# Chosen keys and values brought together by TensorE products with one-hot rows instead of indirect DMA gathers

## The chip, the core and the metric

The kernel runs on one core of a Trainium2 chip. The metric is the time of one execution on the device in microseconds (us), the median of several runs. Lower is better.

## What is computed

One transformer block over 2048 tokens of width 128: a layer norm with a modulation, sparse attention with 16 heads of width 8, then a mixture of eight experts. What matters here is the attention. A small router gives every token a score for every head; in each head only the 819 tokens with the highest scores serve as keys and values (`k_keep`), and all 2048 tokens are queries.

```python
h1 = jax.nn.relu(hidden_states @ r_w1.T + r_b1)
routing_logits = jax.nn.sigmoid(h1 @ r_w2.T + r_b2)
routing_scores = jax.nn.sigmoid(routing_logits)
attn = jnp.einsum('bhqd,bhkd->bhqk', q, k) / jnp.sqrt(jnp.float32(D))
k_keep = max(1, int(tgt_len * SPARSITY))
_, top_idx = jax.lax.top_k(jnp.transpose(routing_scores, (0, 2, 1)), k_keep)
...
sparse = jnp.where(keep[:, :, None, :], attn, NEG_INF)
w = jax.nn.softmax(sparse.astype(jnp.float32), axis=-1).astype(q.dtype)
out = jnp.einsum('bhqk,bhkd->bhqd', w, v)
```

## The kernel before

All five engines run programs written out by hand that meet at semaphores; no scheduler orders anything. The kernel has three parts.

**Ahead of the attention.** Layer norm, the router, keys and values `KV` (tokens on partitions, 32 columns a head pair), queries `QP` in three bf16 parts that sum to the f32 value, and a search in 11 rounds on DVE for each head's threshold. DVE then has, for each token and head, its place among the chosen (L911). From there the chosen keys have to be packed: 819 keys a head make 6 full blocks of 128 and a rest of 51, and the rests of the two heads of a pair (`i`, 0 to 7) share a block, so a pair has `STEPS` = 13 blocks.

To pack them, DVE makes one-hot columns (`columns`, `onehot`, L925 to L939), PE multiplies them (`index_mm`, L1293, then `row_to_partition`, L1304), ACT copies (L684), and DVE writes the row numbers `idx` (`index`, L945). `KV` has meanwhile gone to DRAM (`kv_dram`, L440). POOL then issues one indirect DMA a block (`gathers`, L535), 13 a pair, each fetching 128 rows of 16 f32 values into `G`. `prep` adds the bias and splits the keys into bf16 parts in `KS` (on DVE for pair 0, L972 to L989, on POOL for the others, L552 to L569), `prep_v` puts the values in `VS`, and PE turns `KS` into `KT` (L1413 for pair 0, `turn_k`, L1351, later).

**The attention loop.** A chunk is 512 queries of one pair; there are `NCH` = 32 chunks, four a pair (`NQ`). Two streams run side by side. One finds the largest score of each query: 16 "units" a chunk, each a product of 128 queries with half a head's keys (`score_unit`, L1338 to L1343) into one of three PSUM banks (`RING`) and a maximum over it on DVE (L997). It runs ahead by `LEAD` = 28 units, so that chunk n's loop holds the units of chunks n+1 and n+2. The maxima are split in three bf16 parts by `split_max` in three steps on DVE (L1007, L1011, L1014), turned by PE (`turn_m`, L1357), copied by ACT (`copy_mt`, L695) and carried by SP's DMA into rows of `QS` (`m_rows`, L459). The other stream is the weighting: in `KSTEPS` = 7 steps k, PE computes scores with keys on partitions less the maximum (`scores`, L1382, ended by row parts of `QS`), ACT takes exp (`weights`, L722) into `PR`, and PE multiplies by the values into `OP` (`weigh`, L1398; `weigh_shared`, L1406). ACT copies `OP` to `OS`, PE sums and turns it (`turn_o`, L1362, into a corner of `ST`), ACT copies that (`copy_ot`, L713). PE's program fixes where each of these stands in the row.

POOL's loop over pairs (L585 on) is: `weighted(i - 3)`, which divides a finished pair's output and so waits for DVE's `REC` (L591), then `gathers(i)`, `prep(i)`, `prep_v(i)`. So pair i's gathers (i of 3 and more) are issued from the end of the second chunk of pair i-2 on; those of pairs 0 and 1 stand ahead of the loop, pair 2's at its start. After its last `idx` is ready SP also loads the 4 MB of expert weights (`WE`, L467).

**The tail.** Second layer norm, expert routing, a scatter to slots in DRAM, 24 expert tiles, and a scatter-add to the output.

## Time and profile before

| | us |
|---|---|
| median of 3 runs | 628.78 |
| lowest and highest | 625.04, 629.18 |
| the profiled execution | 629.86 |
| its span in the trace | 628.1 |
| mean granted TensorE clock | 0.793 |

A time of a row is counted from the start of the span. The profiled execution is 1.08 us above the median, and 1.76 us of it lie outside the span.

### The profile page before, as it was taken

To read this page: it belongs to the slowest core of one execution; us is meant where nothing else is said; L and a number is where in the kernel's file an instruction comes from. 1 tells how busy PE (TensorE), PEld (TensorE's weight loads), DVE (VectorE), ACT (ScalarE), POOL (GpSimd) and SP (SyncE) were. 2 spreads that over 40 slices of the span, in tenths; PEclk is the share of its full clock that TensorE was granted. 3 is DMA by queue.
4 is the path that set the end of the run, shared out by engine and by line. 5 is a ranking of instruction groups with operands and counts; after the bars stand their busy time and mean duration, and the time that the engine had idled before them with its cause. 6 is when DMAs were issued, how large, how long until landed. Compare 5 with 4: busy or idle time off the path is not lost.

```text
span 628.1 us, 9542 instructions
## 1 busy us (share of the span) xinstructions
PE 473.5 (75%) x3286; PEld 228.0 (36%) x3286; DVE 392.0 (62%) x1042; ACT 311.9 (50%) x447; POOL 208.6 (33%) x282
## 2 busy tenths in 40 slices
PE   4666526588999599789879969969999976007994
PEld 4334425222333134223223323323434326006993
DVE  8787402675888378468648748737888955202552
ACT  3333000025778267358546637726877873005662
POOL 4100875072003701720640360171000300540886
PEclk9886555557999689779858869878999995557997
DMA  7625000034000010000001001000000001140331
GB/s 229 104 102 147 10 6 4 0 116 160 2 27 3 6 27 2 8 1 28 6 4 27 2 7 28 2 6 12 16 3 2 1 16 54 34 117 18 28 28 12
DMA packets 26346, 22.04 MB, mean 35 GB/s; under 512 B 6272, under 2 KB 22464, under 8 KB 26304
## 3 DMA queue, kind: packets, MB, share of 16 engines
q1 hardware_dynamic: 15632, 16.56, 8.8%
q0 software_dynamic: 7296, 2.96, 4.3%
q10 hardware_dynamic: 3376, 1.98, 1.8%
q8 instruction: 23, 0.38, 0.2%
q14 instruction: 19, 0.16, 0.1%
HBM read 12.89 MB, written 8.93 MB: 35 GB/s over the span
## 4 chain that ended last, share of the span: by engine, by line
PE 58%; DVE 15%; issue 11%; POOL 6%; another core or an unknown queue 5%; ACT 2%; DMA 2%; POOLq 0%; DVEq 0%; SPq 0%; ACTq 0%
PE OP L1398 16%; PE ST L1382 12%; PE SC L1340 6%; DVE tile_max L997 6%; PE ST L1362 5%; POOL out L629 4%; PE SC L1338 4%; PE SC L1293 4%; DVE PR L863 2%; PE OP L1406 2%; POOL slots_dram L621 2%; DMA KV<-slots_dram 1%; PE OP L1479 1%; PE ST L1500 1%
## 5 line engine op out<-in xcount | busy, mean ns | idle before, releaser
L997 DVE TENSOR_REDUCE tile_max<-SC 128x1 f32<-128x410 f32 (+1 forms) x512 | 272.5, 577 | 106.8 <-PE SC L1338 50.8
L722 ACT ACTIVATE PR<-ST 128x1024 f32<-128x1024 f32 (+1 forms) x224 | 209.0, 962 | 84.4 <-PE ST L1382 48.7
L535 POOL DMA_INDIRECT G<-kv_dram,idx x104 | 108.4, 1042 | 79.0 <-DVE idx L945 44.3
L1382 PE MATMUL ST<-QS,KT 51*128 51x512 bf16 (+1 forms) x416 | 118.0, 415 | 12.1 <-issue 7.2
L1398 PE MATMUL OP<-PR,VS 128*32 128x512 f32 x768 | 116.7, 683 | 0.4 <-ACT PR L722 0.4
L1338 PE MATMUL SC<-KT,QS 48*128 48x410 bf16 x256 | 82.7, 378 | 9.8 <-issue 6.2
L1340 PE MATMUL SC<-KT,QS 48*128 48x409 bf16 x128 | 48.8, 381 | 11.5 <-issue 7.6
L1382 PEld LDWEIGHTS ST<-QS,KT 51*128 51x128 bf16 (+1 forms) x416 | 30.7, 98 | 68.6 <-issue 56.6
L1342 PE MATMUL SC<-KT,QS 48*128 48x358 bf16 x128 | 44.6, 348 | 9.9 <-DVE tile_max L997 8.0
L629 POOL DMA_INDIRECT out<-PR,owner x24 | 37.7, 1569 | 28.7 <-issue 27.7
L591 POOL TENSOR_TENSOR XN<-OTS,REC 128x128 f32<-128x128 f32 x14 | 5.5, 414 | 117.0 <-DVE REC L1020 117.0
L1362 PE MATMUL ST<-C,OS 128*128 128x32 f32 x248 | 39.6, 285 | 0.2
L578 POOL COPY VS<-G 128x48 f32<-128x48 f32 x8 | 1.8, 224 | 113.7 <-PE OP L1398 95.7
L1338 PEld LDWEIGHTS SC<-KT,QS 48*128 48x128 bf16 x256 | 19.4, 96 | 50.6 <-DVE tile_max L997 29.6
L1362 PEld LDWEIGHTS ST<-C,OS 128*128 128x128 f32 x248 | 32.9, 194 | 11.6 <-issue 10.8
L1340 PEld LDWEIGHTS SC<-KT,QS 48*128 48x128 bf16 x128 | 12.1, 94 | 66.8 <-DVE tile_max L997 50.4
L695 ACT ACTIVATE MT<-ST 24x128 bf16<-24x128 bf16 x32 | 8.5, 267 | 52.7 <-remote 26.5
L1293 PE MATMUL SC<-ABUF,B 128*14 128x64 f16 x256 | 27.5, 296 | 6.4 <-DVE ABUF L939 3.4
L1500 PE MATMUL ST<-C,KV 128*128 128x128 f32 x24 | 5.9, 428 | 33.9 <-DMA KV<-slots_dram 33.9
L684 ACT ACTIVATE by_code<-SC 14x64 f32<-14x64 f32 x16 | 3.4, 214 | 54.4 <-remote 26.0
L621 POOL DMA_INDIRECT slots_dram<-ABUF,slot x16 | 15.6, 976 | 43.3 <-DVE slot L1163 38.7
L1293 PEld LDWEIGHTS SC<-ABUF,B 128*14 128x14 f16 x256 | 24.0, 109 | 8.8 <-issue 7.4
(240 smaller groups left out, 581.4 us busy)
## 6 DMA issues: line engine op xcount, KB each, us to landing
kv_dram<-KV SPq DMA_DIRECT2D x4, 512.0 KB, 2.9
WE<-in_w_fc SPq DMA_DIRECT2D x1, 2048.0 KB
WE<-in_w_proj SPq DMA_DIRECT2D x1, 2048.0 KB
G<-kv_dram,idx POOLq DMA_INDIRECT x104
slots_dram<-zeros ACTq DMA_DIRECT2D x1, 1548.0 KB, 11.5
KV<-slots_dram SPq DMA_DIRECT2D x1, 1548.0 KB, 7.4
q_parts_dram<-QP SPq DMA_DIRECT2D x3, 512.0 KB, 3.7
QS<-q_parts_dram SPq DMA_DIRECT2D x16, 96.0 KB
```

The lines of the kernel that those rows point to most:

```text
L535: pool.indirect_dma_start(G[:, i % 2, slot_of(s), :], None, kv_dram, bass.IndirectOffsetOnAxis(ap=idx[:, i, s:s + 1].bitcast(U32), axis=0) ...
L621: pool.indirect_dma_start(slots_dram, bass.IndirectOffsetOnAxis(ap=slot[:, t:t + 1].bitcast(U32), axis=0), XN2[:, t, :], None, bounds_chec ...
L629: pool.indirect_dma_start(out[0], bass.IndirectOffsetOnAxis(ap=owner[:, n:n + 1].bitcast(U32), axis=0), YS[:, n, :], None, bounds_check=L ...
L722: nc.scalar.activation(PR[:, k, 0:cols], ST[:, (KSTEPS * n + k) % 2, 0:cols], ACT.Exp, scale=float(D) ** -0.5).then_inc(exp_done, 1)
L997: v.tensor_reduce(tile_max[:, n % 2, at_col:at_col + 1], bank(RING_AT["unit", u])[:, 0:410 - f], AX.X, ALU.max).then_inc(s_reduced, 1)
L1293: last = mm(tokens_of(i)[0][32 * e:32 * e + CODES, :], B1[:, 2 * i + e, t, :], A1[:, i % 2, e, :, t], start=(t == 0), stop=(t == NT - 1), ...
L1338: last = mm(to[:, 0:410], q, KT[rows, i % 2, 0:410], start=True, stop=True)
L1340: last = mm(to[:, 0:409], q, KT[rows, i % 2, 410:KEEP], start=True, stop=True)
L1342: mm(to[:, 0:358], q, KT[rows, i % 2, 410:768], start=True, stop=True)
L1362: last = mm(turned_o(n)[:, 32 * t:32 * t + 32], OS[:, P * t:P * t + P], cc("sum_groups"), start=True, stop=True)
L1382: last = mm(ST[:, at_step % 2, 512 * e:512 * e + 512], KT[rows, i % 2, P * tile:P * tile + P], QS[rows, i % 2, CHUNK * c:CHUNK * (c + 1)], ...
L1398: last = mm(OP[32 * g:32 * g + 32, :], VS[:, i % 2, tile, :], PR[:, k, 512 * e:512 * e + 512], start=first, stop=False, skip_group_check=True)
```

## The change

`kv_dram`, the gathers and the row numbers are gone. A head's 819 keys and values are now brought together on PE: for each of the 16 tiles of 128 tokens there is one product. Its stationary operand is a 128x128 f32 one-hot matrix (token by row within a block), and its moving operand the tile's 16 key and value columns, repeated for each block that the tile can reach and multiplied by 0 or 1 (`masked`), 16 to 112 columns wide; all 16 sum up in one PSUM tile of 112 columns (`bring`). The two heads no longer share the rest block while packing: `SLOTS` = 14.

DVE builds both operands for pair 0. POOL builds them for all others: a head needs four differences of 512 elements a partition, two comparisons of 1024, and three masked products of 256, 896 and 320 (`distances`, `onehot`, `masked`). The operands of pairs 2 to 7 are built during the loop, a half or a whole step beside each chunk (four POOL pieces a pair). The products of pairs 0 and 1 (heads (0,0), (0,1), (1,0), (1,1)) stand ahead of the loop, (1,0) after unit 17 and (1,1) after unit 27. Those of pairs 2 to 7 stand in chunks 1 to 23: 16 in chunk 1, 8 in each of the others, half of them at k=3 and half at k=4. ACT copies the sum out of PSUM (`copy_g`), and `weigh` waits for that, since the sum lies in `OP`'s bank. `turn_o` writes to that bank also, so `weigh` waits for ACT's copy of it, too.

Moved: the second and third step of `split_max` go from DVE to POOL; `turn_m` goes ahead of `turn_o` at k=3; the first `weigh` goes from k=4 to k=5. SP loads `WE` after (1,1) is brought, not after the last `idx`. Buffers of POOL's operands share `ABUF`, `WE` and `QBUF`; the last covers `QP`.

```diff
+FIRST_HALF, SECOND_HALF = range(0, NT // 2), range(NT // 2, NT)
+BRING = {1: (2, 0, range(NT), 0), 2: (2, 1, FIRST_HALF, 0), 3: (2, 1, SECOND_HALF, 1)}
+for p in range(3, NP):
+    for n, (e, part) in enumerate(((0, 0), (0, 1), (1, 0), (1, 1))):
+        BRING[4 * p - 8 + n] = (p, e, [FIRST_HALF, SECOND_HALF][part], part)
...
+        def keys_of(p, e):
+
+            if p == 0:
+                return SC[:, 2 * e, 0:BLOCKS * 2 * D]
+            if p == 1:
+                return ST[:, 1, 512 * e:512 * e + BLOCKS * 2 * D]
+            return OP[:, P:P + BLOCKS * 2 * D]
...
-            for g in range(4):
-                sp.wait_ge(kv_ready, 2 * g + 2)
-                sp.dma_start(kv_t[:, 4 * g:4 * g + 4, :], KV[:, 4 * g:4 * g + 4, :]).then_inc(kv_out, 16)
...
-            sp.wait_ge(idx_ready, NP)
+            sp.wait_ge(g_done, brought(1, 1))
...
-            def gathers(i, tiles=range(STEPS), fetched=gathered):
-                pool.wait_ge(idx_ready, i + 1)
-                if i >= 2:
-                    pool.wait_ge(v_ready, i)
-                    pool.wait_ge(o_norm, 2 * (i - 2))
-                for s in tiles:
-                    pool.indirect_dma_start(
-                        G[:, i % 2, slot_of(s), :], None, kv_dram,
-                        bass.IndirectOffsetOnAxis(ap=idx[:, i, s:s + 1].bitcast(U32), axis=0),
-                        bounds_check=L * H - 1, oob_is_err=False).then_inc(fetched, 16)
...
+            def distances(p, e, first=0, last=NT):
+
+                if p >= 2 and first == 0:
+                    pool.wait_ge(g_done, brought(p - 1 if p > 2 else 0, e))
+                for t in range(first, last, 4):
+                    nc.gpsimd.tensor_tensor(
+                        onehot_of(p, e)[:, t:t + 4, :], cc("place").rearrange("p (a q) -> p a q", a=1).to_broadcast([P, 4, P]),
+                        row_of[:, t:t + 4, 2 * p + e:2 * p + e + 1].to_broadcast([P, 4, P]), ALU.subtract).then_inc(hot_step, 1)
+                    done = next_hot()
+                return done
+
+            def onehot(p, e, done, first=0, last=NT):
+                pool.wait_ge(hot_step, done)
+                for t in range(first, last, 8):
+                    words = onehot_of(p, e)[:, t:t + 8, :]
+                    nc.gpsimd.tensor_scalar(words, words, 0.0, None, ALU.is_equal).then_inc(built, 1)
+
+            def masked(p, e):
+                h = 2 * p + e
+                for t0, t1, b0, b1 in RUNS[e]:
+                    shape = [P, t1 - t0, b1 - b0, 2 * D]
+                    nc.gpsimd.tensor_tensor(
+                        masked_of(p, e)[:, t0:t1, b0:b1, :],
+                        KV[:, t0:t1, 2 * D * h:2 * D * (h + 1)].rearrange("p t (b c) -> p t b c", b=1).to_broadcast(shape),
+                        mask[:, t0:t1, h, b0:b1].rearrange("p t (b c) -> p t b c", c=1).to_broadcast(shape),
+                        ALU.mult).then_inc(built, 1)
+
...
+            def split_max(n):
+
+                part = NMB.rearrange("p (e a t w) -> p e a t w", e=2, a=PARTS, w=2)[:, :, :, :, 1]
+                pool.wait_ge(m_chain, n + 1)
+                nc.gpsimd.tensor_tensor(NM[:, :, 1, :], NM[:, :, 0, :], part[:, :, 0, :], ALU.subtract).then_inc(m_rest, 1)
+                pool.wait_ge(m_rest, n + 1)
+                nc.gpsimd.tensor_tensor(NM[:, :, 2, :], NM[:, :, 1, :], part[:, :, 1, :], ALU.subtract).then_inc(m_split, 1)
...
+                nc.gpsimd.tensor_tensor(g, g, G[:, b, 1, :, :], ALU.add).then_inc(k_step, 1)
...
-            gathers(0, range(EARLY), gathered_early)
-            gathers(0, range(EARLY, STEPS), gathered_late)
-            gathers(1)
-            prep(1)
...
-            for i in range(2, NP):
-                if i >= 3:
-                    weighted(i - 3)
-                gathers(i)
-                prep(i)
-                prep_v(i)
...
+            pool.wait_ge(bias_in, 16)
+            pool.wait_ge(built0, 10)
+            pool.wait_ge(mask_ready, 2)
+            pool.wait_ge(kv_ready, NT // 2)
+            onehot(1, 0, distances(1, 0))
+            masked(1, 0)
+            onehot(1, 1, distances(1, 1))
+            split_max(0)
+            masked(1, 1)
             pool.wait_ge(prepared0, 2)
             prep_v(0)
...
+            pool.wait_ge(qparts_out, 16 * PARTS)
+            for n in range(NCH):
+                i, c = n // NQ, n % NQ
+                if n == 0:
+                    even = distances(2, 0)
+                if n + 1 < NCH:
+                    split_max(n + 1)
+                if c == 0 and i + 1 < NP:
+                    prep(i + 1)
+                    prep_v(i + 1)
+                    if n == 0:
+                        onehot(2, 0, even)
+                        masked(2, 0)
+                    if i + 2 < NP:
+                        onehot(i + 2, 1, distances(i + 2, 1, 0, 8), 0, 8)
+                elif c == 1 and i + 2 < NP:
+                    onehot(i + 2, 1, distances(i + 2, 1, 8, NT), 8, NT)
+                    masked(i + 2, 1)
+                elif c == 2:
+                    if i >= 1:
+                        weighted(i - 1)
+                    if i + 3 < NP:
+                        onehot(i + 3, 0, distances(i + 3, 0, 0, 8), 0, 8)
+                elif c == 3 and i + 3 < NP:
+                    onehot(i + 3, 0, distances(i + 3, 0, 8, NT), 8, NT)
+                    masked(i + 3, 0)
...
+            def copy_g(p, e, part, number):
+
+                act.wait_ge(g_done, number)
+                if p == 0 and e == 0:
+                    act.wait_ge(init_pool, 1)
+                if p >= 2:
+                    act.wait_ge(v_ready, 3 * (p - 1))
+                src = keys_of(p, e).rearrange("p (b c) -> p b c", b=BLOCKS)
+                to = G[:, p % 2, part, :, :]
+                if e == 0:
+                    nc.scalar.activation(to[:, 0:13:2, :], src, ACT.Copy).then_inc(g_copied, 1)
+                else:
+                    nc.scalar.activation(to[:, 1:12:2, :], src[:, 1:, :], ACT.Copy).then_inc(g_first, 1)
+                    nc.scalar.activation(to[:, 13, :], src[:, 0, :], ACT.Copy).then_inc(g_copied, 1)
...
-                if n >= 1:
-                    act.wait_ge(otr_done, n)
                 if n + 1 < NCH:
                     copy_mt(n + 1)
+                if n in BRING:
+                    act.wait_ge(g_done, brought_by(n))
                 if n >= 1:
                     copy_ot(n - 1)
+                if n in BRING:
+                    p, e, tiles, part = BRING[n]
+                    copy_g(p, e, part, brought_by(n))
                 weights(n, 4, 3)
                 weights(n, 5, 4)
...
+            masks(0, 2)
+            dve.wait_ge(kv_ready, NT // 2)
+            dve.wait_ge(mask_ready, 1)
+            for e in range(2):
+                onehot(e)
+                masked(e)
...
+            def bring(p, e, tiles, begins=True, ends=True):
+
+                if p == 0:
+                    pe.wait_ge(built0, 5 * (e + 1))
+                else:
+                    pe.wait_ge(built, 5 * (2 * (p - 1) + e + 1))
+                for t in tiles:
+                    b0, b1 = reach(t, e)
+                    last = mm(keys_of(p, e)[:, 2 * D * b0:2 * D * b1], onehot_of(p, e)[:, t, :],
+                              masked_of(p, e)[:, t, b0:b1, :].rearrange("p b c -> p (b c)"),
+                              start=(begins and t == tiles[0]), stop=(ends and t == tiles[-1]), skip_group_check=True)
+                return last
...
-                    if k == 5 and n >= 1:
-                        pe.wait_ge(ot_ready, n)
...
+                    pe.wait_ge(v_ready, 3 * (i + 1))
                     if n >= 1:
-                        pe.wait_ge(o_copied, n)
+                        pe.wait_ge(ot_ready, n)
+                    pe.wait_ge(g_copied, brought_by(n))
...
+            bring(0, 1, range(NT)).then_inc(g_done, 1)
+            turn_first(0, SC[0:64, 1, :])
...
+            for u in range(12, 18):
                 score_unit(u)
-            pe.wait_ge(q_ready, 4 * PARTS)
+            bring(1, 0, range(NT)).then_inc(g_done, 1)
+            for u in range(18, LAST[0] + 5):
+                score_unit(u)
             turn_m(0)
             for u in range(LAST[0] + 5, LEAD):
                 score_unit(u)
...
+                    scores(n, k, 0 if k == 3 else e, True)
+                    unit()
                     if k == 3:
-                        scores(n, k, 0, True)
+                        if n + 1 < NCH:
+                            turn_m(n + 1)
                         unit()
                         if n >= 1:
                             turn_o(n - 1, (0, 1))
-                        unit()
-                        if n >= 1:
+                            unit()
                             turn_o(n - 1, (2, 3))
-                        if n + 1 < NCH:
-                            turn_m(n + 1)
+                        if n in BRING:
+                            p, e_, tiles, part = BRING[n]
+                            bring(p, e_, tiles[:len(tiles) // 2], ends=False)
                         continue
-                    scores(n, k, e, True)
-                    unit()
                     scores(n, k, 1 - e, False)
+                    if k == 4 and n in BRING:
+                        p, e_, tiles, part = BRING[n]
+                        bring(p, e_, tiles[len(tiles) // 2:], begins=False).then_inc(g_done, 1)
+                    if k == 5:
+                        weigh(n, (0, 1), first=True)
+                    if k == 6:
+                        weigh_shared(n)
                     unit()
                     if k == 1:
...
                     if k == 2 and n % NQ == 1 and n // NQ + 1 < NP:
                         turn_k(n // NQ + 1)
-                    if k == 4:
-                        weigh(n, (0, 1), first=True)
-                        unit()
-                    if k == 5:
-                        weigh_shared(n)
+                while units:
+                    unit()
                 weigh(n, (2, 4))
```

What stands in PE's row in a chunk, from k=3 to the first `weigh`. Before (`ST<-QS,KT` are `scores`, `SC<-KT,QS` units, `OS` is `turn_o`, `NM` is `turn_m`, `OP<-PR,VS` is `weigh`):

```order
L1362 MATMUL ST<-C,OS 128x32 x2
L1357 MATMUL ST<-identb,NM 24x128
L1382 MATMUL ST<-QS,KT 128x512
L1338 MATMUL SC<-KT,QS 128x410
L1382 MATMUL ST<-QS,KT 128x512
L1342 MATMUL SC<-KT,QS 128x358
L1343 MATMUL SC<-KT,QS 128x51
L1398 MATMUL OP<-PR,VS 32x512 x4
```

And of the change, in a chunk whose first eight tiles are brought (`OP<-QBUF,ABUF` are the products of `bring`):

```order
L1377 MATMUL ST<-identb,NM 24x128
L1358 MATMUL SC<-KT,QS 128x410
L1382 MATMUL OP<-C,OS 128x32 x2
L1358 MATMUL SC<-KT,QS 128x410
L1382 MATMUL OP<-C,OS 128x32 x2
L1325 MATMUL OP<-QBUF,ABUF 128x32
L1325 MATMUL OP<-QBUF,ABUF 128x48
L1325 MATMUL OP<-QBUF,ABUF 128x64
L1325 MATMUL OP<-QBUF,ABUF 128x80
L1400 MATMUL ST<-QS,KT 128x512
L1362 MATMUL SC<-KT,QS 128x358
L1363 MATMUL SC<-KT,QS 128x51
```

`turn_m` now stands ahead of both parts of `turn_o`; four products follow them, and after the next two `scores` come four more.

POOL's row for one pair in the loop before (`G` gathered, then the bias and the split into `KS`):

```order
L535 DMA G<-kv_dram,idx 128x16 x13
L552 TENSOR_TENSOR G<-G,BG 128x208
L556 CAST KS<-G 128x13x24
L558 TENSOR_TENSOR KR<-G,KS 128x104
L560 CAST KS<-KR 128x13x16
L562 TENSOR_TENSOR KR<-KR,KS 128x104
```

And in the change, from the end of `prep` in a pair's first chunk to the second `split_max` after it (`ABUF` one-hot rows, `QBUF` masked columns, `NM` `split_max`):

```order
L601 COPY VS<-G 128x7x8
L602 COPY VS<-G 128x6x8
L603 COPY VS<-G 128x8
L536 TENSOR_TENSOR ABUF<-C,row_of 128x512 x2
L546 TENSOR_SCALAR ABUF<-ABUF 128x1024
L562 TENSOR_TENSOR NM<-NM 128x2x4
L564 TENSOR_TENSOR NM<-NM 128x2x4
L536 TENSOR_TENSOR ABUF<-C,row_of 128x512 x2
L546 TENSOR_SCALAR ABUF<-ABUF 128x1024
L552 TENSOR_TENSOR QBUF<-KV,mask 128x4x80
L552 TENSOR_TENSOR QBUF<-KV,mask 128x896
L552 TENSOR_TENSOR QBUF<-KV,mask 128x4x64
```

The 13 DMAs are gone; elementwise work of each chunk stands between one chunk's `split_max` and the next one's.

## Rows read from the trace of the kernel before

**Rows 1.** Busy time of each engine in stretches (us, instructions), PEclk, DMA share, GB/s.
```profile
208.00:224.00 16.00, 9.72 (x47) 2.27 (x43) 6.06 (x12) 5.37 (x7) 8.91 (x14) 0.50 0.06 5
432.00:448.00 16.00, 15.89 (x131) 6.49 (x131) 14.25 (x34) 12.49 (x19) 0.82 (x4) 1.00 0.10 26
```
**Rows 2.** Timeline of ACT, `copy_mt` alone: start, us, what, idle before.
```profile
196.21 0.27 ACT L695 ACTIVATE MT<-ST 24x128 bf16<-24x128 bf16 x1 [0.69 <-PE ST L1362]
209.87 0.27 ACT L695 ACTIVATE MT<-ST 24x128 bf16<-24x128 bf16 x1 [3.04 <-remote]
227.87 0.27 ACT L695 ACTIVATE MT<-ST 24x128 bf16<-24x128 bf16 x1 [0.86 <-PE ST L1362]
```
**Rows 3.** Timelines: POOL's split beside DVE's maxima, then one pair's gathers on POOL.
```profile
155.89 0.58 DVE L997 TENSOR_REDUCE tile_max<-SC 128x1 f32<-128x409 f32 x1
...
156.02 0.38 POOL L558 TENSOR_TENSOR KR<-G,KS 128x104 f32<-128x104 f32 x1
...
199.05 1.06 POOL L535 DMA_INDIRECT G<-kv_dram,idx  x1 [0.85 <-POOL XN L591]
...
214.76 1.00 POOL L535 DMA_INDIRECT G<-kv_dram,idx  x1 [0.30 <-issue]
```
**Rows 4.** Timeline, all engines, from the places to the loop's first `scores`.
```profile
53.59 0.62 DVE L925 TENSOR_TENSOR WE<-key_of,C 128x448 f16<-128x448 f16 x1
...
61.88 2.95 POOL L535 DMA_INDIRECT G<-kv_dram,idx  x1 [44.34 <-DVE idx L945]
...
102.10 0.87 POOL L558 TENSOR_TENSOR KR<-G,KS 128x104 f32<-128x104 f32 x1
...
114.48 0.85 PE L1413 MATMUL SC<-identb,KS 128*64 128x128 bf16 x6 [2.19 <-DVE RS L989]
...
116.24 0.50 PE L1338 MATMUL SC<-KT,QS 48*128 48x410 bf16 x1 [0.80 <-DVE KT L991]
...
135.74 0.61 PE L1382 MATMUL ST<-QS,KT 51*128 51x512 bf16 x1 [1.61 <-DMA QS<-MT]
```
**Rows 5.** Timeline of PE and DVE in a chunk without gathers.
```profile
468.37 0.39 PE L1382 MATMUL ST<-QS,KT 51*128 51x512 bf16 x1
...
472.01 0.63 PE L1362 MATMUL ST<-C,OS 128*128 128x32 f32 x4
...
472.58 0.34 PE L1338 MATMUL SC<-KT,QS 48*128 48x410 bf16 x1
...
477.85 0.39 PE L1382 MATMUL ST<-QS,KT 51*128 51x512 bf16 x1
...
471.60 0.16 DVE L1007 TENSOR_REDUCE NM<-tile_max 128x8 f32<-128x16 f32 x1
```
**Rows 6.** A stretch of the tail, a PE row, and groups by form (the first from 432 to 500).
```profile
592.00:608.00 16.00, 16.00 (x142) 15.84 (x142) 10.19 (x27) 10.50 (x18) 13.37 (x9) 1.00 0.35 30
...
566.98 5.94 PE L1500 MATMUL ST<-C,KV 128*128 128x128 f32 x24 [33.91 <-DMA KV<-slots_dram]
...
L1340 PEld LDWEIGHTS SC<-KT,QS 48*128 48x128 bf16 x28 | 2.6, 92 | 12.1 <-DVE tile_max L997 12.1
...
L615 POOL TENSOR_TENSOR KV<-XN,gate 128x448 f32<-128x448 f32 x4 | 4.4, 1138 | 0.1
L1044 DVE TENSOR_TENSOR X<-KV,X 128x1792 f32<-128x1792 f32 x1 | 2.0, 2018 | 0.0
...
L521 POOL CAST place<-C 128x1024 f16<-128x1024 f32 x1 | 1.0, 1037 | 0.1
```
**Rows 7.** The load of `WE`: SP's issue, a stretch, the second chunk's first `scores`.
```profile
134.98 0.57 SPq L467 DMA_DIRECT2D WE<-in_w_proj  x1
...
148.00:150.00 2.00, 2.00 (x13) 0.27 (x9) 1.10 (x3) 1.02 (x1) 0.62 (x1) 0.50 0.13 46
...
150.39 0.60 PE L1382 MATMUL ST<-QS,KT 51*128 51x512 bf16 x1
```

405 lines of the change are left out of this document (158 added, 247 removed).

## The prediction, made before the changed kernel was timed

> **What bounds the kernel now.** I read the stretches of busy time first, then one engine's timeline, then the places where a stretch falls out of the pattern. In the loop there are two kinds of stretch. In a quiet one PE is busy 15.9 of 16 us, DVE 14.3, and the granted clock is 1.00; in one with gathers PE is busy 9.7, DVE 6.1 and the clock is 0.50, which is 1.2 GHz [rows 1]. A quiet chunk takes 9.48 us from its first `scores` to the next one's (468.37 to 477.85) [rows 5]. ACT copies one `MT` a chunk, so its marks give the length of others: 209.87 - 196.21 = 13.66 and 227.87 - 209.87 = 18.00 around the gathers [rows 2]. The 13 gathers run from 199.05 to 215.8, back to back [rows 3]. In that time ACT's wait of 3.04 us ends with "remote" [rows 2], so with no event of another engine, and after them the clock has fallen. A pair's gathers so cost 13.66 + 18.00 - 2 x 9.48 = 12.7 us. Five pairs (3 to 7) have theirs in the loop: 64 us. I read this as cause and effect, since quiet chunks differ in nothing else.
>
> Ahead of the loop the path is: places ready at 53.6, first gather at 61.9, the 26 gathers of pairs 0 and 1 until pair 1's keys are split at 102.1, first unit at 116.24, first `scores` of the loop at 135.74, where PE had waited 1.61 us for `QS<-MT` [rows 4]. PE is nearly idle during those gathers.
>
> A quiet chunk is bound by PE and DVE together. `turn_o` takes 0.57 a half (472.01 to 472.58), and DVE's negated maximum of the chunk starts 3.23 us after the chunk does [rows 5]. PE's loads for units wait 12.1 us for DVE's maxima in 68 us, 7.2 chunks, so 1.7 a chunk [rows 6].
>
> **The head of the kernel.** Gone: index products, gathers and their landing, from 53.6 to the first unit. Added on DVE: an elementwise operation of two inputs costs 2.02 / 1792 = 1.13 ns an element [rows 6]. Masks of two heads (224 elements) 0.4, a head's one-hot rows 2 x 1.2, its masked columns (1472 elements in three) 1.8. Head (0,0) is built at 53.6 + 4.6 = 58.2, (0,1) at 62.4, beside PE's work on the first.
>
> PE's price: 142 records in 16 us at clock 1.00, two records a product, so 0.225 us for a 128x128 by 128 f32 product; and 12 f32 turns (24 records) in 5.94 us, 0.495 each, in a stretch behind an idle one, so I read them as cold [rows 6]. The new products are narrower (16 to 112 columns), but `turn_o`, with 32 columns and the same 128x128 f32 stationary side, still takes 0.285 each [rows 5]. So width saves nothing, and I take 0.225 at the full clock and 0.495 at half. A head (16 products) costs 3.6 to 7.9 us. For pair 0 I take one head cold and one warm, 11.5 us, since PE comes from an almost idle stretch and is then dense: done at 69.7. From the turn of the keys to the first unit 1.8 us pass now (114.48 to 116.24) [rows 4], so the first unit is at 71.5. From there to the loop are 19.5 us now; the 1.6 us wait for `MT` is covered by the heads put between, and these add 13 us (both behind sparse units, so mostly cold; 7.2 to 15.8) and 0.6 for the last copy. The loop starts at 71.5 + 17.9 + 13.6 = 103.0 instead of 135.7: **-33 us**. All warm it would be -43, all cold -26.
>
> POOL must keep up. Two inputs cost it (1138 - 380) / (448 - 104) = 2.2 ns an element and 0.15 us an instruction [rows 3, 6]: 512 elements 1.28, the masked ones 0.71, 2.12 and 0.85. The comparison with a constant on POOL has no row: at least the cast of as many elements with one input, 1.04, at most the two-input price, 2.4; I take 1.04, the same size and count of inputs. A head is 4 x 1.28 + 2 x 1.04 + 3.7 + 0.6 between them = 11.5 (14.2 at the upper end). It starts at 64, so (1,0) is ready at 76, well before PE asks at about 84. (1,1)'s masked part stands behind `split_max(0)`, which waits for unit 19, and is ready at about 97, when PE arrives: no cost, 2 us at worst.
>
> The Trainium skill, "GPSIMD Engine Reference", section 4.1, advises against just this: elementwise work belongs on VectorE, GpSimd being about 2x slower with two inputs and near line rate with one. The trace agrees on the first (2.2 against 1.13 ns) [rows 6]. It has no row for the second, and by the page the comparison would stay near the low end.
>
> **Chunk 0.** It lasts 14.65 us now (135.74 to 150.39) with the load of `WE` in it [rows 4, 7]. The load is issued at 134.98 and over at about 148.3, since the stretch from 148 carries only 46 GB/s; the second chunk's `MT` rows are behind it in SP's queue. With the issue 0.6 us ahead of the loop the chunk cannot be shorter than about 13.3: **-1 us**, no more, though the pair-2 gathers have left it.
>
> **The other chunks.** The gathers' 12.7 us go five times: **-64 us**. What comes in, by walking through PE's new row with the durations of the quiet chunk:
> - 8 products: 8 x 0.225 and 0.12 for each of two starts, 2.04 us. PE has 1.7 us of waits a chunk, but while PE runs products or `weigh` DVE drains its three banks in 1.5 us and idles, so I hide nothing.
> - `turn_m` now comes about 3.64 us into the chunk. DVE's maximum ends at 3.39, two POOL subtractions of 0.16 with 0.07 between handoffs end at 3.9: PE waits 0.26. Queued behind it are all units and so DVE.
> - `weigh` at k=5 waits for two or three ACT copies behind the second half of the products (0.2 to 0.25 each), about 0.2 more than what PE has between. ACT's later exps have room: it works 7.5 of 12 us.
> - Half of the products and `weigh` now stand close together, with DVE idle; its lag costs a last 0.05.
>
> So a chunk with 8 products lasts 12.0, +2.5; one without, 9.8, +0.3; chunk 1, with 16, +4.4. In the five later chunks with a `turn_k`, that covers the 0.26. Sum: 4.4 + 22 x 2.5 + 6 x 0.3 - 1.3 = **+60 us**. For 0.1 us of error a chunk the sum moves by 2.3. Bounds: +1.2 a chunk where DVE's share hides the rest, +3.5 where each wait is twice its size.
>
> POOL's load a pair in the loop: two heads 23.0, `prep` 3.8 (7 operations of 112 to 336 elements), values 0.8, `weighted` 0.8, four `split_max` 1.9: 30.3 of 48.5 us, and at most 10 in a chunk of 12, so each `split_max` finds POOL free; in chunk 1, after a backlog of 13 us, it may come 1.5 late.
>
> The tail is unchanged: 0. Sum against the profiled execution: 629.9 - 33 - 1 - 64 + 60 = 591.9. The median shown is 1.1 lower, so **591 us**.
>
> **The rivals.**
> - *The products hide in PE's and DVE's waits.* If the products fall in PE's 1.7 us of waits, a chunk costs +1.2: 22 x 1.3 = 29 less, 562. Against it: those waits stand at k=1 and k=3, the products behind `turn_o`.
> - *A new wait a chunk.* `OP`'s bank now passes `turn_o`, ACT's copy, products, ACT's copy and `weigh` in a row, and ACT stands still until the products end. If a chunk loses 1 us more, exp and `scores` follow: 591 + 23 = 614.
> - *POOL becomes the bound, slower than before.* While DVE ran f16 operations with two SBUF inputs, POOL's 104-element operation took 0.87 us, in the loop 0.38 [rows 3, 4], a factor of 2.3. If DVE's maxima held up the now constant POOL work so, a pair would need 70 us of POOL against 48.5: 21.5 x 5.5 pairs more, 709 us. It turns slower than before from a factor of 1.8 on (30.3 to 55 us). Against it: in the loop DVE reads PSUM, and the 0.38 stand beside such a maximum [rows 3]. The Trainium skill, "Advanced Engine Details and Errata", section "VectorE Performance Modes", says that the second Vector SBUF port is shared with GPSIMD so that the two block each other. The row at 102.10 agrees; the row at 156.02, beside a reduction from PSUM, shows none of it.
> - *The stalls don't come from the gathers.* Then 64 us stay: 655. Chunks without gathers show none, so little speaks for it.
>
> **How the numbers follow.** Forecast 0.54 (own range 575 to 606), hidden products 0.16, new wait 0.22, POOL the bound 0.05, stalls stay 0.03. The range from 564 to 614 takes in most of the second and third and leaves some 0.17 out. A measurement of this kernel can tell about 1% from no change. Faster by over 1%: 0.90; within 1%: 0.02 (the third case far worse than worked out); slower: 0.08.
>
> **What would show it.** First unit near 71 and the loop's first `scores` near 103; `MT` marks 12.0 us apart in chunks 2 to 23 with none of 13.7 and 18.0 behind each other, 9.8 after; clock 1.00 through the loop; no "remote" waits but in chunk 0; `bring` records at 0.11 us. Wrong would be: marks 11 or 13 apart, PE waiting long for `built` or `m_split` (POOL), or a loop start after 110.

## The result and the profile after

The changed kernel takes 652.94 us (median of 4 runs, 651.28 to 657.0) against 628.98 beside it: ratio 1.0393, 95% interval 1.0317 to 1.047. The forecast was 591, its range 564 to 614. The profiled execution took 651.28 us, its span is 649.4.

The page of the changed kernel, its first two parts (busy time of each engine; the span in 40 slices of 16.2 us, tenths):

```profile
PE 543.5 (84%) x3510; PEld 291.3 (45%) x3510; DVE 385.0 (59%) x957; ACT 306.9 (47%) x472; POOL 283.9 (44%) x353
...
PE   4776589799999999999999999999999997005994
...
PEclk9786665667987979877797987979796795557998
```

PE is busy from one end of the loop to the other, and yet its clock goes up and down in a regular pattern. The head of the kernel came as forecast. PE's timeline of the changed kernel there (start, length, line; answers to [rows 4]):

```profile
57.14 10.34 PE L1325 MATMUL SC<-PR,ABUF 128*128 128x16 f32 x64 [5.44 <-DVE PR L989]
...
70.16 0.33 PE L1358 MATMUL SC<-KT,QS 48*128 48x410 bf16 x1 [0.80 <-DVE KT L1033]
...
104.84 0.61 PE L1400 MATMUL ST<-QS,KT 51*128 51x512 bf16 x1 [0.42 <-ACT G L729]
```

The first unit stands at 70.16 (forecast 71.5; 116.24 before), the loop's first `scores` at 104.84 (forecast 103.0; 135.74 before). The loss is in the loop. ACT's copies of `MT`, one a chunk, in pair 3 (answer to [rows 2]):

```profile
190.82 0.25 ACT L741 ACTIVATE MT<-ST 24x128 bf16<-24x128 bf16 x1
202.40 0.25 ACT L741 ACTIVATE MT<-ST 24x128 bf16<-24x128 bf16 x1
217.47 0.25 ACT L741 ACTIVATE MT<-ST 24x128 bf16<-24x128 bf16 x1
```

11.58 us, then 15.07. From chunk 3 on, such marks lie 11.6 to 12.2 apart in about every second chunk, as forecast (12.0), and 15.0 to 16.0 in most of the others. The stretch at 202 shows what the long ones have. PE's timeline, then the stretches of busy time around it (in each: length, busy us and instructions of PE, PEld, DVE, ACT and POOL, granted clock, DMA share, GB/s):

```profile
202.01 0.23 PE L1377 MATMUL ST<-identb,NM 128*24 128x128 bf16 x1 [0.29 <-POOL NM L564]
202.17 0.34 PE L1358 MATMUL SC<-KT,QS 48*128 48x410 bf16 x1
202.45 0.63 PE L1382 MATMUL OP<-C,OS 128*128 128x32 f32 x4
203.01 0.34 PE L1358 MATMUL SC<-KT,QS 48*128 48x410 bf16 x1
203.28 0.90 PE L1382 MATMUL OP<-C,OS 128*128 128x32 f32 x4
203.99 1.97 PE L1325 MATMUL OP<-QBUF,ABUF 128*128 128x32 f32 x8
...
206.78 2.05 PE L1325 MATMUL OP<-QBUF,ABUF 128*128 128x96 f32 x8
```

```profile
198.00:202.00 4.00, 3.61 (x29) 1.18 (x25) 3.32 (x8) 3.39 (x5) 0.44 (x3) 1.00 0.01 4
202.00:206.00 4.00, 3.99 (x21) 3.37 (x22) 1.95 (x4) 0.65 (x3) 3.91 (x5) 0.69 0.01 2
206.00:210.00 4.00, 4.00 (x20) 2.28 (x23) 1.27 (x3) 1.14 (x4) 1.57 (x1) 0.50 0.00 0
210.00:214.00 4.00, 4.00 (x38) 1.05 (x30) 2.44 (x5) 2.61 (x4) 0.00 (x0) 0.96 0.01 2
```

Four turns of `OS` with 32 columns (the second pair 0.90 in place of 0.63), then four products in 1.97 us, where in the next chunk, at the full clock, four take 1.10: the clock has gone from 1.00 to 0.50 (1.2 GHz) in the midst of records that follow each other without a gap. Read in stretches of 0.5 us from the loop's first `scores` (104.84) to its last `weigh` (533.1), the clock stood at 0.50 for 139.5 us of 428, in 16 spells; 14 of them, 7 us or longer each, lie behind chunk 1. "Low for so many us" below is always counted like this, within the loop. No engine's wait explains it: in the whole execution PE waited 8.0 us for `split_max`, and POOL stood idle for 233 us, waiting for DVE's maximum:

```profile
POOL NM L562 <- DVE NM L1047: 233.2, 31, 13.9
...
PE ST L1377 <- POOL NM L564: 8.0, 24, 1.3
```

So the rival with POOL as the bound is out. What remained was: why does the clock fall in this row, when in a quiet chunk before, with the same four narrow turns, it stayed at 1.00 [rows 1, 5]? It isn't the products alone: it also falls in three of the last eight chunks, which have none (their marks are 14.0 to 15.0 apart, beside 9.3 to 9.9 for their neighbours). PE's timeline in one of these; the second pair of turns is again the one that takes longer:

```profile
485.25 0.23 PE L1377 MATMUL ST<-identb,NM 128*24 128x128 bf16 x1 [0.28 <-POOL NM L564]
...
485.68 0.63 PE L1382 MATMUL OP<-C,OS 128*128 128x32 f32 x4
...
486.52 0.83 PE L1382 MATMUL OP<-C,OS 128*128 128x32 f32 x4
```

### The profile page after: what moved, and what is told of

Its sections match the earlier page's. It is cut to its first block, busy times and chain, and to the rows that moved or that the text cites. A ratio compares the mean times of both kernels' runs of the same rounds, so it can differ in the third digit from the quotient of the medians.

```text
span 649.4 us, 9915 instructions
## 1 busy us (share of the span) xinstructions
PE 543.5 (84%) x3510; PEld 291.3 (45%) x3510; DVE 385.0 (59%) x957; ACT 306.9 (47%) x472; POOL 283.9 (44%) x353
## 4 chain that ended last, share of the span: by engine, by line
PE 66%; DVE 14%; POOL 9%; issue 7%; ACT 2%; DMA 2%; POOLq 0%; DVEq 0%; ACTq 0%
PE OP L1417 16%; PE OP L1325 11%; PE ST L1400 8%; PE OP L1382 6%; PE SC L1358 5%; DVE tile_max L1039 4%; PE SC L1360 4%; POOL out L668 2%; PE SC L1534 2%; PE ST L1325 2%; PE ST L1544 2%; PE OP L1425 2%; POOL slots_dram L660 2%; DVE PR L913 1%; POOL ABUF L546 1%
## 5 line engine op out<-in xcount | busy, mean ns | idle before, releaser
L1325 PE MATMUL OP<-QBUF,ABUF 128*128 128x112 f32 (+6 forms) x384 | 73.9, 353 | 0.0
L1325 PEld LDWEIGHTS OP<-QBUF,ABUF 128*128 128x128 f32 x384 | 66.5, 262 | 8.1 <-issue 7.6
L546 POOL TENSOR_SCALAR ABUF<-ABUF 128x1024 f32<-128x1024 f32 x24 | 66.5, 2770 | 1.9
L759 ACT ACTIVATE OTS<-OP 128x128 f32<-128x128 f32 x32 | 8.9, 278 | 123.3 <-PE OP L1325 114.3
L1358 PEld LDWEIGHTS SC<-KT,QS 48*128 48x128 bf16 x256 | 19.1, 95 | 70.1 <-DVE tile_max L1039 44.8
L536 POOL TENSOR_TENSOR ABUF<-C,row_of 128x512 f32<-128x512 f32 x48 | 49.2, 1047 | 0.0
L1382 PE MATMUL OP<-C,OS 128*128 128x32 f32 x256 | 42.4, 292 | 0.8 <-ACT OS L752 0.7
L1382 PEld LDWEIGHTS OP<-C,OS 128*128 128x128 f32 x256 | 35.4, 201 | 13.1 <-issue 11.0
L552 POOL TENSOR_TENSOR QBUF<-KV,mask 128x256 f32<-128x256 f32 (+2 forms) x36 | 35.7, 1020 | 0.0
L1417 PEld LDWEIGHTS OP<-PR,VS 128*32 128x32 f32 x768 | 16.6, 115 | 33.8 <-issue 32.2
```

What stands on the lines that cost most here:

```text
L536: nc.gpsimd.tensor_tensor(onehot_of(p, e)[:, t:t + 4, :], cc("place").rearrange("p (a q) -> p a q", a=1).to_broadcast([P, 4, P]), row_of[: ...
L546: nc.gpsimd.tensor_scalar(words, words, 0.0, None, ALU.is_equal).then_inc(built, 1)
L1325: last = mm(keys_of(p, e)[:, 2 * D * b0:2 * D * b1], onehot_of(p, e)[:, t, :], masked_of(p, e)[:, t, b0:b1, :].rearrange("p b c -> p (b c) ...
L1358: last = mm(to[:, 0:410], q, KT[rows, i % 2, 0:410], start=True, stop=True)
L1382: last = mm(turned_o[:, 32 * t:32 * t + 32], OS[:, P * t:P * t + P], cc("sum_groups"), start=True, stop=True)
L1417: last = mm(OP[32 * g:32 * g + 32, :], VS[:, i % 2, tile, :], PR[:, k, 512 * e:512 * e + 512], start=first, stop=False, skip_group_check=True)
```

## The experiments

Each kernel was timed beside the kernel before on the same chip, and ratios are to it. The experiments come in five groups. Where I compare medians between groups, it is of versions without gathers in the loop: the changed kernel (653, 650, 649 us) and the one with 128 columns (608.4 twice) repeat within 1% from group to group.

**First group: the order, the width, the handoff, the products.** The kernel before took 632.78 us beside these four.

`e1_turn_m_behind`:
```diff
-                        if n + 1 < NCH:
-                            turn_m(n + 1)
                         unit()
                         if n >= 1:
                             turn_o(n - 1, (0, 1))
                             unit()
                             turn_o(n - 1, (2, 3))
+                        if n + 1 < NCH:
+                            turn_m(n + 1)
```


> The changed kernel with `turn_m` put back behind the second half of `turn_o`, as before the change; nothing else. Theory A (TensorE's granted clock falls in a stretch in which PE streams few columns: the f32 turns of `OS` with 32 columns and the products with 16 to 112, side by side): both still stand together, so the clock still falls to 0.50 in about every second chunk, and the time is 640 to 655. Theory B (what lets the clock fall is PE's 0.28 us wait for `m_split`, which now stands ahead of `turn_o`): `turn_m` comes 1.1 us later and waits for nothing, the clock stays at 1.00 in the loop, and the time is 595 to 605. Theory C (the clock isn't the cause at all, the chunk is longer by DVE's or POOL's share): no change beyond the wait, 645 to 655 with marks of `MT` as they are now.

650.63 us, ratio 1.0277 (1.0207 to 1.0347). PE no longer waits at `turn_m`, and the clock was low for 136 us, nearly as long as with the wait. Theory B is out: the 0.29 us of idleness don't bring the clock down.

`e2_wide_columns`:
```diff
-                    b0, b1 = reach(t, e)
+                    b0, b1 = [run[2:] for run in RUNS[e] if run[0] <= t < run[1]][0]
```


> The changed kernel with each product's moving side as wide as its run of blocks (64, 112 and 80 columns, 80 and 64 for the ends) in place of the 16 to 112 columns that the tile can reach; the added columns are zeros, the output is the same. The count of instructions is the same. Theory A (few columns let the clock fall): the stretch has about half as many columns again, the clock falls in fewer chunks or none, and the time is 600 to 630 although each product does more. Theory B (PE's wait for `m_split`): the wait is unchanged, so the clock falls as often, 652 to 660. Theory C (clock not the cause): the products cost the same or more, 652 to 665.

651.27 us, ratio 1.0283 (1.0251 to 1.0315), low for 134 us. Outside theory A's range; by itself this spoke against it. The added columns lie in the products alone, behind the turns at which the clock had fallen in the rows above. So the width of the products isn't what decides.

`e3_split_on_dve`:
```diff
+                dve.wait_ge(m_chain, n + 1)
+                v.tensor_tensor(NM[:, :, 1, :], NM[:, :, 0, :], part[:, :, 0, :], ALU.subtract).then_inc(m_rest, 1)
+                dve.wait_ge(m_rest, n + 1)
+                v.tensor_tensor(NM[:, :, 2, :], NM[:, :, 1, :], part[:, :, 1, :], ALU.subtract).then_inc(m_split, 1)
...
-                if n + 1 < NCH:
-                    split_max(n + 1)
```


> The changed kernel with both subtractions of `split_max` on DVE directly behind its negated maximum, no handoff to POOL. Theory A (few columns): PE's wait at `turn_m` is shorter by 0.1 to 0.2 us a chunk, 3 to 6 us in all, and the clock falls nearly as often, so 640 to 652. Theory B (the wait lets the clock fall): about 600. Theory C: 647 to 650, the wait alone. POOL's place in the time, if it has one, would show here as well.

682.88 us, ratio 1.0818 (1.0778 to 1.0858): 30 us slower, missed by every theory. DVE's timeline of this kernel at one `split_max`:

```profile
305.43 0.16 DVE L1044 TENSOR_REDUCE NM<-tile_max 128x8 f32<-128x16 f32 x1
305.63 0.65 DVE L1051 TENSOR_TENSOR NM<-NM 128x8 f32<-128x8 f32 x1
306.31 0.97 DVE L1053 TENSOR_TENSOR NM<-NM 128x8 f32<-128x8 f32 x1
```

The same two subtractions took 0.16 each in the kernel before (median of 32), and in most chunks here they do so too. In 9 of 32 chunks the first, or both, fall beside POOL's building of operands and take four to six times as long. POOL's timeline at the same place shows what they wait for:

```profile
305.21 2.05 POOL L536 TENSOR_TENSOR ABUF<-C,row_of 128x512 f32<-128x512 f32 x2
307.35 2.78 POOL L546 TENSOR_SCALAR ABUF<-ABUF 128x1024 f32<-128x1024 f32 x1
```

POOL's two subtractions, halves of the 2.05 us, end near 306.2 and 307.3, DVE's at 306.28 and 307.28: each of DVE's ends where one of POOL's does. Beside a comparison of POOL's (205.62 to 208.39) the first takes 1.00, and the second, which starts 1.09 us into it, 0.17. PE waits for them at `turn_m` in these 9 chunks, up to 1.42 us and 10.9 us in all, and the clock was low for 168 us, 28.5 more than in the changed kernel; at half the clock that would be worth some 14 us (an estimate). So the longer waits explain 11 of the 30 us, the clock most of the rest. DVE's subtractions on SBUF do suffer from POOL, and the changed kernel's own place for them, on POOL, is the better one.

`e4_two_products`:
```diff
-                            bring(p, e_, tiles[:len(tiles) // 2], ends=False)
+                            bring(p, e_, tiles[:1], ends=False)
...
-                        bring(p, e_, tiles[len(tiles) // 2:], begins=False).then_inc(g_done, 1)
+                        bring(p, e_, tiles[-1:], begins=False).then_inc(g_done, 1)
```


> Leaves out, in the chunks of the loop, all products of a half but its first and its last tile (6 of 8; 14 of 16 in chunk 1), so most keys and values of pairs 2 to 7 are not brought together. Everything else, copies and waits included, is the changed kernel's. By the working of the prediction the left-out products cost 6 x 0.225 = 1.35 us a chunk in 22 chunks, and 3.2 in chunk 1: 33 us. Theory A (few columns): the sparse stretch is shorter by that, the clock falls more seldom, so the gain is 33 and a good part of the 50 us that I put on the clock: 570 to 605. Theory B (the wait at `turn_m`): the clock falls as often, 33 us less, 620. Theory C (not the clock): 620 as well, or 635 if the products were half hidden.

608.5 us, ratio 0.9623 (0.9588 to 0.9657), just above theory A's range. Chunks at the full clock have marks 10.8 apart in place of 12.15: six products are 1.34 us, 0.22 each where the forecast had 0.225. The clock still falls as often as before (18 spells in the loop, 102 us in all, most of them shorter), so the products alone are not what lets it fall.

**Second group: fill the columns.** The kernel before took 549.77 us beside these four, and not 633. I come to that below; here the variants are compared with one another and with the changed kernel of the other groups.

`e5_full_turn_o` (and `e7_full_both` in addition: `masked_of(p, e)[:, t:t + 1, b0:b1, :]` broadcast twice for tiles of up to four blocks):
```diff
-                    last = mm(turned_o[:, 32 * t:32 * t + 32], OS[:, P * t:P * t + P], cc("sum_groups"),
+                    last = mm(OP[:, 32 * t:32 * t + P].rearrange("p (a c) -> p a c", a=4), OS[:, P * t:P * t + P],
+                              cc("sum_groups").rearrange("p (a c) -> p a c", a=1).to_broadcast([P, 4, 32]),
```


> The changed kernel with the moving side of each f32 turn of `OS` repeated four times (128 columns in place of 32, by a broadcast of `sum_groups`); the surplus columns are overwritten or unused, the output is the same, and so is the count of instructions. Theory A (TensorE's granted clock falls where few columns are streamed): the four turns a chunk stream four times as many columns in nearly the same time, since the 128x128 f32 load sets their pace, so the clock falls in fewer chunks, in the plain chunks at the end above all (three falls now): 620 to 645. Theory D (the clock falls by how little PE works in all, whatever the columns): nothing changes, 650 to 657.

> As the run before, and the moving side of each product of pairs 2 to 7 with up to 64 columns repeated twice (the second copy lands in unused columns of `OP`); same output, same count of instructions, more work for PE. Theory A: the loop's clock stays at 1.00 nearly throughout, each product takes 0.225 to 0.25 us, and the time is 597 to 620, so more work makes the kernel faster. Theory D: no faster, 650 to 665.

608.44 us (607.22 to 608.69) and 607.03 (606.0 to 607.67). From the end of chunk 1 to the end of the loop the clock never leaves 1.00 in either. The first is even below theory A's range. The second, with wider products besides, gains nothing clear over it: again the width of the turns counts, that of the products doesn't.

`e6_before_no_gathers` (of the kernel before):
```diff
-                for s in tiles:
+                for s in tiles if i < 3 else ():
...
-                pool.wait_ge(gathered, 16 * (STEPS * i))
+                pool.wait_ge(gathered, 16 * (STEPS * min(i, 2)))
```


> The kernel before, with the gathers of pairs 3 to 7 left out (POOL's other work on them, waits included, stays; those pairs compute on the keys and values of earlier pairs). The prediction's step: the five pairs' gathers cost 64 us by stalls and by the clock, so 629 - 64 = 565, every chunk 9.5 to 10.3 us, clock 1.00. If instead the clock falls by what PE streams, gathers or not, and only the stalls of ACT and PE with the release "remote" are the gathers': clock falls stay in some chunks, 575 to 600.

552.53 us, ratio 1.0054 (1.0021 to 1.0088): here the gathers cost nothing. It was outside both ranges. And without any gather near, the clock still fell once behind chunk 1, for 3.5 us from 331.5 on.

`e8_spread` (`some(1)` is one product of the half; the other edits move the first `weigh` to k=6 and ACT's copy behind exp of k=4):
```diff
                     scores(n, k, 0 if k == 3 else e, True)
+                    if k in (4, 5):
+                        some(1)
                     unit()
+                    if k in (4, 5):
+                        some(1)
```


> The changed kernel with the 8 products of a chunk set one at a time between units and `scores` of k=3 to 5, and the first `weigh` at k=6 together with `weigh_shared`; ACT copies the brought halves one exp later. Same instructions, other order. Theory A (sparse stretch): no stretch of the chunk is sparse any more, the clock falls seldom, 600 to 625. Theory D: 645 to 660. A new wait (ACT's copies ahead of the first `weigh`, or exp of k=5 behind them) would add 0.3 to 0.8 us a chunk, 7 to 18 us.

773.39 us. The opposite of what I expected: the clock was low for 298.5 us, in every chunk with products. My picture of one sparse spot that could be thinned out was wrong.

**Third group: both kernels and both keys once more, on one chip.** The kernel before took 625.65 us beside these.

> The kernel before, unchanged, run for its trace: beside the last four kernels it took 550 us, beside the four ahead of them 633. Theory E (the 80 us are what gathers and their stalls cost, and how much that is varies with the chip the kernels run on): where it takes 550, its `MT` marks are 9.5 to 10.3 us apart, gathers or not, and no wait ends with "remote"; where it takes 630, chunks with gathers take 13.7 to 18. Theory F (the 80 us have another source, the clock by itself): the marks are longer in chunks without gathers too.

> The changed kernel, unchanged, beside the kernel before and the one with full turns on the same chip. Theory A (few columns let the clock fall, on any chip): 645 to 660, some 17 falls of the clock, and the run with 128 columns in `turn_o` 40 to 50 us faster. Theory G (the falls came from the chip and not from the columns): about 608 where the kernel before takes 550, no falls, and full turns bring nothing.

> The changed kernel with 128 columns in each turn of `OS`, again, now beside the changed kernel itself. Theory A: 605 to 612 on any chip, the loop's clock at 1.00. Theory G: the same as the changed kernel, whatever that takes.

> The kernel before with the gathers of pairs 3 to 7 left out, again, beside the kernel before. Theory E: 550 to 555 on any chip; where the kernel before takes 630, that is 80 us less, where it takes 550, nothing. Theory F: where the kernel before takes 630, this one takes 600 or more.

| kernel | us | ratio, 95% |
|---|---|---|
| before | 628.96 | 1.0019 (0.9968 to 1.0071) |
| changed | 650.02 | 1.0372 (1.0267 to 1.0477) |
| changed, 128 columns in `turn_o` | 608.4 | 0.9747 (0.9667 to 0.9826) |
| before, no gathers of pairs 3 to 7 | 571.09 | 0.9145 (0.9066 to 0.9224) |

The third is faster than the kernel before, but whether by more than 2% the interval leaves open. Against the changed kernel it has the same count of instructions, 96 surplus columns in each of four turns, and takes 42 us less. The slices and PE's timeline of the third (the same chunk as in the rows at 202 above):

```profile
PEclk9887755668999999999999999999999985558998
```

```profile
195.72 0.23 PE L1377 MATMUL ST<-identb,NM 128*24 128x128 bf16 x1 [0.29 <-POOL NM L564]
195.88 0.34 PE L1358 MATMUL SC<-KT,QS 48*128 48x410 bf16 x1
196.15 0.71 PE L1382 MATMUL OP<-C,OS 128*128 128x128 f32 x4
196.79 0.34 PE L1358 MATMUL SC<-KT,QS 48*128 48x410 bf16 x1
197.07 0.71 PE L1382 MATMUL OP<-C,OS 128*128 128x128 f32 x4
197.62 1.01 PE L1325 MATMUL OP<-QBUF,ABUF 128*128 128x32 f32 x8
```

The wait of 0.29 is still there; each pair of turns costs 0.08 more, and four products take 1.01 where they took 1.97. Theories C, D and G don't hold. Of theory A this much is shown: with more columns in the four turns, and nothing else changed, the clock stays up. The wide form, few columns anywhere in the row, isn't: wider products did nothing. Which of the row's other moves brought the falls about, when the kernel before has turns as narrow and hardly any falls without gathers, was not tested one by one, except `turn_m`'s place, and that isn't it (`e1_turn_m_behind`). So that stays open. The Trainium skill, "TensorE: Matmul & The Clock Gate", section "HAM oscillation — how this bites in real kernels", puts the rule as leaving PE no idle gaps. By that rule this row was safe: PE's longest steady wait is 0.3 us in both. The trace doesn't agree that this is enough: in the rows above PE was busy 3.99 of 4 us while the clock fell.

Theory F is out, and theory E's cause holds: the marks of the loop span 368.7 us in the kernel before here and 304.1 without the gathers of five pairs. Its size was wrong. I expected 550 to 555 and 80 us less; it is 571.09, 55 to 58 less. The gathers of pairs 0 to 2 are still in, and those ahead of the loop stall here as before: the first `MT` mark stands at 133.88, and at 114.23 in `e6_before_no_gathers`.

**Fourth group: what was still open.** The kernel before took 549.7 us beside these.

`f1_spread_full` is `e8_spread` with the edits of `e7_full_both`.


> The order of the run with products spread over k=3 to 5, which took 773 with the clock low from one end of the loop to the other, and both columns of `turn_o` and of the products filled up as in the run with both full. If that run was slow because thin streams among the dense ones leave no stretch dense enough (Theory A, mended): full columns bring the clock back to 1.00 and the time to 608 to 620. If it was slow by its order and its waits, with the clock only following: over 680.

693.06 us, in the range of the second reading. Full columns take back 80 us all the same, with the clock low for 100.5 us and not 298.5. The other 86 us over `e7_full_both`, which has the same columns in blocks, are order: a product by itself between bf16 matmuls, here with 128 columns, takes 0.42 us (306.48 to 306.90 in its timeline, at clock 1.00) and not 0.225, marks lie 14.3 apart at the full clock, and the clock still falls in places, though the columns are filled. So few columns are not the only thing that lets it fall.

`f3_turn_o_64` is `e5_full_turn_o` with the columns repeated twice in place of four times.


> The changed kernel with 64 columns in each turn of `OS` (32 take 650, 128 take 608). Theory A: a time between, with fewer falls than 17: 610 to 640. A threshold that 64 columns already pass would show as 608.

637.08 us, low for 102.5 us (139.5 with 32 columns, 22.5 to 26.5 with 128, all of these in chunks 0 and 1). A value between, as theory A had it, and no step at 64.

`f2_full_and_start`: `e5_full_turn_o`, and
```diff
+                if n in (5, 6):
+                    sp.wait_ge(g_done, brought(1, 1))
+                    sp.dma_start(WE[:, :, HD * (n - 5):HD * (n - 4)], [w_fc, w_proj][n - 5].rearrange("n p c -> p n c"))\
+                        .then_inc(we_in, 16)
...
-                    if i + 2 < NP:
+                    if i + 2 < NP and n > 0:
                         onehot(i + 2, 1, distances(i + 2, 1, 0, 8), 0, 8)
                 elif c == 1 and i + 2 < NP:
+                    if n == 1:
+                        onehot(i + 2, 1, distances(i + 2, 1, 0, 8), 0, 8)
```


> The kernel with 128 columns in `turn_o`, with its two early waits taken away: the two loads of `WE` are issued behind the `MT` rows of chunks 6 and 7 in place of chunk 0's start (PE's 1.80 us for `QS<-MT`), and POOL's first half of one-hot rows (2,1) stands behind `split_max(2)` in place of ahead of it (PE's 2.04 us for `m_split`). Theory A: 3.8 us of waits, and the clock, which those two idle stretches kept at 0.50 from 107 to 141 us but for a few, comes back earlier, 3 to 6 us more: 598 to 602. If the low clock there came from the thin stream of chunk 1's 16 products, only the waits go: 604 to 605.

601.99 us, in theory A's range. PE's wait for `QS<-MT` is gone, the one for `m_split` in chunk 1 fell only from 2.04 to 1.47, the clock is low in the loop for 16.5 us, and in chunk 1 it falls as before:

```profile
120.00:123.00 3.00, 1.53 (x9) 0.83 (x8) 1.32 (x3) 1.50 (x3) 2.92 (x6) 1.00 0.00 0
123.00:126.00 3.00, 3.00 (x19) 2.89 (x19) 0.58 (x1) 0.00 (x0) 2.91 (x2) 0.72 0.01 2
126.00:129.00 3.00, 3.00 (x15) 2.20 (x14) 0.58 (x1) 0.00 (x0) 2.91 (x4) 0.50 0.00 0
```

The fall comes among the 16 narrow products, but PE had also been idle for half of the 3 us ahead of them, so this run can't tell which of the two let the clock fall here.

**Fifth group: the kernel before where it takes 550.** It took 550.16 us beside these.

> The kernel before, unchanged, for its trace on one more chip. It took 629, 633 and 626 us on some chips and 550 on two others. Where it takes 550: `MT` marks of 9.5 to 10.3 us in chunks with gathers too, no wait that ends with "remote" on ACT or DVE, and the loop's first `MT` mark near 114 in place of 132. Where it takes 630: as the trace already seen.

> The changed kernel, unchanged. 645 to 655 on either kind of chip, since it has no gathers in the loop and its clock falls by what PE streams: against the kernel before 1.03 to 1.05 on the one kind, 1.17 to 1.19 on the other.

> 128 columns in `turn_o` and the two early waits taken away, again: 600 to 604 on either kind of chip; where the kernel before takes 626 to 633, 4 to 5% faster than it, where it takes 550, 9 to 10% slower.

| kernel | us | ratio, 95% |
|---|---|---|
| before | 550.25 | 0.9998 (0.997 to 1.0027) |
| changed | 649.06 | 1.1779 (1.1699 to 1.186) |
| `f2_full_and_start` | 601.07 | 1.0896 (1.0808 to 1.0984) |

POOL's timeline of the kernel before in this group, first and last of pair 3's 13 gathers, and ACT's marks around them:

```profile
179.84 1.06 POOL L535 DMA_INDIRECT G<-kv_dram,idx  x1 [0.85 <-POOL XN L591]
...
195.51 1.00 POOL L535 DMA_INDIRECT G<-kv_dram,idx  x1 [0.30 <-issue]
```

```profile
176.78 0.27 ACT L695 ACTIVATE MT<-ST 24x128 bf16<-24x128 bf16 x1 [0.81 <-PE ST L1362]
187.62 0.27 ACT L695 ACTIVATE MT<-ST 24x128 bf16<-24x128 bf16 x1 [0.86 <-PE ST L1362]
197.10 0.27 ACT L695 ACTIVATE MT<-ST 24x128 bf16<-24x128 bf16 x1 [0.86 <-PE ST L1362]
```

The gathers stand one behind the other at the same pace as in [rows 3], with the same durations, and the chunks beside them take 10.84 and 9.48 us where [rows 2] has 13.66 and 18.00. No wait of the whole execution ends with "remote". So on this chip the same gathers stall nobody, in the loop or ahead of it: the first `MT` mark is at 114.22 here and at 132.5 in the profile shown. The groups in which the kernel before took about 630 and those in which it took 550 ran on different chips, and the one chip that came twice gave 550 both times. The changed kernel takes 649 to 653 on both kinds, the one with 128 columns 608.4 on both. What differs between the chips was not found.

## Why the prediction was wrong, point by point

- **Head of the kernel, -33.** Right: first unit 70.16 for 71.5, loop at 104.84 for 103.0. Two terms inside it missed, both small. Pair 0's products took 10.34 us for 11.5, those of the two heads behind 6.20 and 7.01, inside the 3.6 to 7.9. The first miss: POOL's comparison, taken at 1.04 us, took 2.77, outside my bound of 2.4:

```profile
L546 POOL TENSOR_SCALAR ABUF<-ABUF 128x1024 f32<-128x1024 f32 x24 | 66.5, 2770 | 1.9
```

  It cost PE nothing here. A head took POOL 12.6 us (62.94 to 75.56), inside my 11.5 to 14.2, since a subtraction of 512 took 1.05 for 1.28, and POOL then stood idle for 8.71 us ahead of `split_max(0)`. PE's one wait for it, 1.00 us ahead of the fourth head, comes from the masked part that stands behind `split_max(0)`, where I had put nothing, 2 us at worst. The Trainium skill, "GPSIMD Engine Reference", section 4.1, has one-input operations near line rate; the row is at 2.7 ns an element, above the two-input 2.0 (1047 for 512, line L536). The second miss: DVE's small operations of `prep`, 0.2 to 0.3 us each in the kernel before, took 0.8 to 1.1 beside POOL; my forecast had nothing for that.
- **Chunk 0, -1.** Right: 13.71 us from its first `scores` to the next chunk's (104.84 to 118.55), 13.65 forecast.
- **Gathers, -64.** The size is right on chips of the kind that the profile shows: the loop's marks span 368.7 us with them and 304.1 without, 64.6; by the medians it is 55 to 58. The words "quiet chunks differ in nothing else" were too strong: on the other kind the gathers are there and the stalls are not, so gathers are needed for the stalls but don't make them alone. And `e6_before_no_gathers` lost the clock once with no gather near.
- **Other chunks, +60.** This is the step that failed: with the rest of the sum as measured (31 for the head, 1, 64), it was 117. Its parts were right: 0.22 a product, marks of 12.1 and 11.6 for 12.0 in chunks at full clock, 9.86 for 9.8 without products, 0.29 for the wait of 0.26, 0.17 for the wait on ACT's copies. What was wrong was one premise, stated as "clock 1.00 through the loop": I walked through PE's new row with durations read at clock 1.00 and took the clock as given, because the kernel before had lost it, as I read it, only beside gathers. In its place the clock fell in about every second chunk, and each fall cost 2.7 to 4.0 us (5.5 once) against the same chunk with wider turns; wider turns alone gave back 42 us, with the same instructions and nearly the same waits.
- **Chunk 1.** Forecast with 16 products at +4.4. It took 24.64 us (118.55 to 143.19), about 10 more than forecast, with the clock low from end to end. PE waited 1.30 us for `m_split` in it, inside the 1.5 that the forecast allows, so the wait isn't what it had wrong. `f2_full_and_start` took back 6.4 us of this start.
- **Rivals.** POOL as the bound: out, 233 us idle. Its mechanism was seen all the same, the other way round: POOL slows DVE's SBUF operations (`e3_split_on_dve`), not DVE POOL. I had cited the Trainium skill, "Advanced Engine Details and Errata", for it; by its section "GPSIMD Details" the two share a read and a write interface, and conflict where DVE's instruction has two SBUF inputs. These subtractions have two, and the rows agree: 0.65 and 0.97 for 0.16, each until POOL's own subtraction ends. New wait a chunk: out, it was 0.29. Products hidden: out. "The stalls stay", 655, names nearly the right time for a wrong reason: there is no "remote" wait in the loop any more.

The sum: 592 forecast, 42 that the wider turns gave back, 9 for what chunk 1 lost even with them, 2 for the head and some 6 by which chunks with wider turns at the full clock are longer than forecast, makes 651; the profiled execution is 651.28. Of those 6, some 3 to 5 are the price of the surplus columns themselves (0.08 us a pair of turns), which the changed kernel doesn't pay, so the low clock behind chunk 1 cost it about 45 to 47 us and not 42 (an estimate from the marks).

The fastest version without gathers is `f2_full_and_start`, 601 to 602 us. It was timed only where the kernel before takes 550, and is 9 to 10% slower there. Where that one takes 626 to 633, only `e5_full_turn_o` was timed beside it (0.9747), so that `f2_full_and_start` would be faster still is likely and not shown. Where the gathers stall nobody, the kernel before stays the best of all.

## What to carry to other kernels

A row of matmuls can be busy without a gap and still lose the clock. Where an edit adds narrow f32 matmuls or moves them, price the stretch at the lower clock too, and try surplus columns on each kind of them: on the four turns they cost 0.08 us a pair and gave back 42 us in all, on the products they gave nothing. Durations read at one clock hold only as long as the new row keeps that clock. A stall that the profile puts down to no engine should be seen on a second chip before a step rests on it.
